# Local attention on one core: both band copies on VectorE, both probability scalings on GpSimd, the logarithm and exponential of the lengths moved behind the next tile's squares

## What is computed

```python
h = shift_token(x)
q, k, v = split(h @ wqkv)                    # 8 heads of 64
q, k = l2norm(q) * qs, l2norm(k) * ksc       # t / |t|
q, k = rotary_xpos(q, k)
sim = einsum(8 * q, look_around(k))          # windows of 64, this one and the one before
sim = where(i < j or i > j + 64 or j == -1, -big, sim)
attn = softmax(sim)
x = x + (attn @ look_around(v)) @ wo
# then a gated feed-forward layer with a layer norm ahead of it
```

## Time and profile before

| | us |
|---|---|
| median of three runs | 2175.28 |
| the profiled execution | 2175.47 |
| its span, first to last instruction | 2173.7 |
| PE busy | 2061.9 (95%) |
| DVE busy | 1712.6 (79%) |
| ACT busy | 1567.4 (72%) |
| POOL busy | 1514.7 (70%) |

### The profile page before, as it was taken

How to read it: one execution, slowest core, us unless ns; L and a number is a source line. 1 busy time by engine, 2 the same in 40 slices (tenths; PEclk the granted TensorE clock), 3 DMA queues, 4 the chain that set the end, 5 groups by cost and what they waited for, 6 DMA issues and landing times.

```text
span 2173.7 us, 53335 instructions
## 1 busy us (share of the span) xinstructions
PE 2061.9 (95%) x18830; PEld 1419.0 (65%) x18846; DVE 1712.6 (79%) x4035; ACT 1567.4 (72%) x4511; POOL 1514.7 (70%) x1837
## 2 busy tenths in 40 slices
PE   6999889999999999899999999999999989999988
PEld 4777657776567776565666666665777756677755
DVE  6787679998579999667766777677999956999965
ACT  3665569999459999436566556656999954999962
POOL 6788878887157777358787787876887833777742
PEclk9999999999999999999999999999999999999999
DMA  4000012112211121121121121210112121111211
GB/s 122 1 1 1 7 22 45 39 31 50 52 28 42 39 49 43 49 71 55 42 59 32 50 60 40 57 28 21 33 39 46 43 51 26 39 40 41 46 36 51
DMA packets 121369, 88.35 MB, mean 41 GB/s; under 512 B 85561, under 2 KB 102161, under 8 KB 118801
## 3 DMA queue, kind: packets, MB, share of 16 engines
q1 hardware_dynamic: 118544, 82.69, 15.8%
q10 hardware_dynamic: 2560, 2.24, 0.4%
HBM read 30.38 MB, written 8.39 MB: 18 GB/s over the span
## 4 chain that ended last, share of the span: by engine, by line
PE 60%; POOL 11%; DVE 11%; issue 7%; ACT 5%; SPq 4%; DMA 2%; POOLq 0%; ACTq 0%; DVEq 0%
PE bank L1379 11%; PE bank L620 7%; PE bank L1390 5%; PE bank L1370 5%; PE bank L687 5%; PE bank L662 4%; PE bank L633 4%; PE bank L675 4%; PE bank L695 3%; PE bank L750 3%; PE bank L627 3%; SPq L475 3%; POOL store L1178 2%; ACT store L874 2%; PE bank L758 2%
## 5 line engine op out<-in xcount | busy, mean ns | idle before, releaser
L1486 ACT ACTIVATE store<-bank 128x512 f32<-128x512 f32 x512 | 286.9, 600 | 201.6 <-PE bank L1379 198.4
L1533 DVE CUSTOM_DVE_ANT_0 store<-bank,store 128x512 f32<-128x512 f32 x512 | 335.7, 688 | 119.7 <-PE bank L1370 66.7
L1606 POOL TENSOR_SCALAR store<-store 128x512 f32<-128x512 f32 x512 | 349.6, 697 | 108.2 <-DVE store L1533 106.6
L874 ACT ACTIVATE store<-bank,store 128x128 f32<-128x128 f32 x1024 | 365.5, 385 | 16.7 <-DVE store L1030 16.3
L1178 POOL TENSOR_TENSOR store<-store 128x512 f32<-128x512 f32 x254 | 318.1, 1273 | 31.8 <-DVE store L1019 27.4
L1191 POOL TENSOR_TENSOR store<-store 128x512 f32<-128x512 f32 x256 | 261.8, 1044 | 111.5 <-ACT store L513 111.5
L1379 PEld LDWEIGHTS bank<-store 128*128 128x128 f32 x2048 | 239.8, 141 | 133.6 <-ACT store L1486 75.7
L1379 PE MATMUL bank<-store 128*128 128x128 f32 x2048 | 298.5, 277 | 0.0
L620 PE MATMUL bank<-store 128*128 128x512 f32 x496 | 234.8, 594 | 3.2 <-DVE store L1019 3.0
L874 ACT ACTIVATION_READ_ACCUMULATOR store<-bank,store 128x1 f32 x1024 | 228.9, 224 | 0.0
L1182 POOL TENSOR_TENSOR store<-store 128x512 f32<-128x512 f32 x128 | 133.3, 1041 | 126.4 <-DVE store L1035 126.4
(11 more groups left out here) (229 smaller groups left out, 4577.3 us busy)
## 6 DMA issues: line engine op xcount, KB each, us to landing
store<-store SPq DMA_DIRECT2D x256, 128.0 KB, 2.4
store<-parts SPq DMA_DIRECT2D x96, 192.0 KB
parts<-store SPq DMA_DIRECT2D x16, 384.0 KB, 3.6
store<-store SPq DMA_DIRECT2D x128, 32.0 KB
store<-store SPq DMA_DIRECT2D x128, 31.8 KB
store<-store SPq DMA_DIRECT2D x32, 127.0 KB
store<-in_L_ffn_wqkv_dram SPq DMA_DIRECT2D x4, 768.0 KB, 4.2
out_dram<-store SPq DMA_DIRECT2D x8, 256.0 KB, 2.4
```

The source lines that it names most:

```text
L874: last = nc.scalar.activation(prob[:, e, b, :], bank[3 + e][:, b * P:(b + 1) * P], ACT.Exp, bias=nmax[:, e, b:b + 1], accum_out=psums[:, e ...
L1486: nc.scalar.activation(AT[:, h % 4, c, :], bank[SCORE_BANKS + (64 * q + 4 * h + c) % TURN_BANKS][:, :], ACT.Exp, scale=-1.0).then_inc(aexp ...
L1533: nc.vector.tensor_tensor_reduce(out=S[:, h % 4, t, :], in0=bank[(64 * q + 4 * h + t) % SCORE_BANKS][:, :], in1=decay[:, off:off + L], sca ...
L1606: nc.gpsimd.tensor_scalar(s_, s_, -1.0, amax[:, h % 4, t:t + 1], ALU.mult, ALU.add).then_inc(shifted_done, 1)
```

## The change

Three steps. ScalarE no longer writes the band of bank 3; VectorE writes both bands, one after the other, behind `inverse_sums(j, 1)`. VectorE no longer scales the odd heads' probabilities; GpSimd scales both halves, the second one between `add_turned` and `clip_lengths` of `finish_qk`. And `inverse_lengths(j+2)`, which stood at the end of tile j, now stands in tile j+1 between `squares(j+3)` and `exps(j+1, 0)`.

```diff
@@ ScalarE
-            def write_band(q, j):
-                act.wait_ge(exp_done, 8 * q + 2 * j + 1)
-                nc.scalar.activation(bank[3][:, :], band_b[...], ACT.Copy).then_inc(band_at[0], 1)
...
+                    lengths = (q, j + 1) if j < 3 else (q + 1, 0)
+                    if (j == 0 and not before) or (j == 3 and not more):
+                        lengths = None
                     if more or j < 2:
                         ahead = (q, j + 2) if j < 2 else (q + 1, j - 2)
                         squares(*ahead)
+                    if lengths:
+                        inverse_lengths(act, *lengths)
                     exps(q, j, 0)
...
                         copy_v(*ahead)
-                    if more or j < 3:
-                        write_band(*((q, j + 1) if j < 3 else (q + 1, 0)))
                     copy_pT(q, j, 0)
-                    if more or j < 2:
-                        inverse_lengths(act, *ahead)
@@ VectorE
-            def scale_probs(q, j, e):
-                dve.wait_ge(pinv_done[e], 4 * q + j + 1)
-                nc.vector.tensor_tensor(prob[:, e, :, :], ...).then_inc(scaled_p[e], 1)
-            def write_band(q, j):
-                dve.wait_ge(exp_done, 8 * q + 2 * j + 2)
-                nc.vector.tensor_copy(bank[4][:, :], band_b[...]).then_inc(band_at[1], 1)
+            def write_band(q, j, e):
+                dve.wait_ge(exp_done, 8 * q + 2 * j + e + 1)
+                nc.vector.tensor_copy(bank[3 + e][:, :], band_b[...]).then_inc(band_at[e], 1)
...
                     inverse_sums(q, j, 1)
                     if more or j < 3:
-                        write_band(*((q, j + 1) if j < 3 else (q + 1, 0)))
-                    scale_probs(q, j, 1)
+                        write_band(*((q, j + 1) if j < 3 else (q + 1, 0)), 0)
+                        write_band(*((q, j + 1) if j < 3 else (q + 1, 0)), 1)
@@ GpSimd
-            def scale_probs(q, j):
+            def scale_probs(q, j, e):
...
             def finish_qk(q, j, first=False, added=False, between=None):
                 if not added:
                     add_turned(q, j, 0)
                     add_turned(q, j, 1)
+                if between:
+                    scale_probs(*between, 1)
                 if not first:
                     clip_lengths(q, j)
...
-                    scale_probs(q, j)
+                    scale_probs(q, j, 0)
                     if more or j < 2:
-                        finish_qk(*((q, j + 2) if j < 2 else (q + 1, j - 2)))
+                        finish_qk(*((q, j + 2) if j < 2 else (q + 1, j - 2)), between=(q, j))
+                    else:
+                        scale_probs(q, j, 1)
```

More of the change, by code:

```diff
@@ L876, in exps @@
                 last.then_inc(exp_done, 1)
-            def write_band(q, j):
-                act.wait_ge(exp_done, 8 * q + 2 * j + 1)
-                nc.scalar.activation(bank[3][:, :], band_b[:, 0 if j else 2, :, :].rearrange("p b w -> p (b w)"),
-                                     ACT.Copy).then_inc(band_at[0], 1)
             def copy_pT(q, j, e):
@@ L1035, in inverse_sums @@
                 nc.vector.reciprocal(pinv[:, e, :], psums[:, e, :]).then_inc(pinv_done[e], 1)
-            def scale_probs(q, j, e):
-                dve.wait_ge(pinv_done[e], 4 * q + j + 1)
-                nc.vector.tensor_tensor(prob[:, e, :, :], prob[:, e, :, :], bc(pinv[:, e, :], 2, P), ALU.mult).then_inc(scaled_p[e], 1)
-            def write_band(q, j):
-                dve.wait_ge(exp_done, 8 * q + 2 * j + 2)
-                nc.vector.tensor_copy(bank[4][:, :], band_b[:, 0 if j else 2, :, :].rearrange("p b w -> p (b w)")).then_inc(band_at[1], 1)
+            def write_band(q, j, e):
+                dve.wait_ge(exp_done, 8 * q + 2 * j + e + 1)
+                nc.vector.tensor_copy(bank[3 + e][:, :], band_b[:, 0 if j else 2, :, :].rearrange("p b w -> p (b w)")).then_inc(band_at[e], 1)
             def add_out(s, q, j):
@@ L1178, in add_turned @@
                 nc.gpsimd.tensor_tensor(straight[:, at, :], straight[:, at, :], turned[:, at, :], ALU.add).then_inc(add_done, 1)
-            def scale_probs(q, j):
-                pool.wait_ge(pinv_done[0], 4 * q + j + 1)
-                nc.gpsimd.tensor_tensor(prob[:, 0, :, :], prob[:, 0, :, :], bc(pinv[:, 0, :], 2, P), ALU.mult).then_inc(scaled_p[0], 1)
+            def scale_probs(q, j, e):
+                pool.wait_ge(pinv_done[e], 4 * q + j + 1)
+                nc.gpsimd.tensor_tensor(prob[:, e, :, :], prob[:, e, :, :], bc(pinv[:, e, :], 2, P), ALU.mult).then_inc(scaled_p[e], 1)
             def normalize(q, j, i):
@@ L1198, in clip_lengths, with finish_qk @@
                 nc.gpsimd.tensor_scalar(flat, flat, 1e-24, None, ALU.max).then_inc(clip_done, 1)
-            def finish_qk(q, j, first=False, added=False):
+            def finish_qk(q, j, first=False, added=False, between=None):
                 if not added:
```

## The result

| | before | after |
|---|---|---|
| median of four runs each, side by side | 2175.61 | 2188.89 |
| lowest and highest | 2174.26, 2177.27 | 2188.59, 2189.79 |
| the profiled execution | 2175.47 | 2189.15 |
| its span | 2173.7 | 2187.0 |
| mean granted clock of TensorE | 0.996 | 0.992 |

A forecast was written before the change was run, and what follows sets the result against it. The prediction took a ring of waits through ScalarE and TensorE, 7.94 us per tile, to bound the kernel. Its terms, -4.6 + 8.4 + 2.2 - 0.8 = +5.2 us, gave 2180.5, range 2169 to 2190.

The forecast's parts named there:

- What bounds the tile: Ordinary tile: a ring of waits sets its 7.94 us, and TensorE's 0.17 idle ahead of the scores awaits ScalarE's band copy.
- both rings: Two loops of waits, each 7.94 us: one through ScalarE's copy_pT and first exponential, one through its band copy and the scores.
- Ordinary tiles, -4.6: 92 tiles away from layers' starts, ends and the power: each gains 0.05 us, 4.6 us in all.
- ScalarE's ring: Loop from copy_pT through the first exponential, weigh_values and prob_transpose: shrinks from 7.94 to 7.89 us.
- Rival 2: Ordinary tiles: the scores' ring rules and weigh_values waits for VectorE; tile 7.77 us, total 2169.5; chance 0.08.
- rival 3: GpSimd becomes the pacemaker: second scaling 1.25 us, clip still 0.68; total 2188, or 2197 without slack; chance 0.12.
- The band copies hidden: VectorE's second band copy ends at 709.21, wanted at 709.33: 0.1 us of slack, so no cost.
- Logarithm at 1.45, clip at 0.25, scaling at 1.04: Ordinary tile: logarithm starts 1.45 us after copy_pT; on GpSimd the clip takes 0.25 and the second scaling 1.04.
- The 12 tiles, 8.82 and +8.4: Tiles with the layer norm's power: late clip delays the logarithm; 8.82 us against 8.15, 8.4 us lost in all.
- Rival 1: Tiles with the layer norm's power: the late clip costs no more than before; total 2170 to 2172; chance 0.17.
- Layers' ends, +2.2: Last tile's odd scaling and the power for ff_normalize come later on GpSimd: +0.55 us each, 2.2 in all.
- Layers' starts, -0.8: VectorE, 0.6 us lighter, gives back an estimated 0.2 us at each layer's start, 0.8 in all.

The follow-up runs named there:

- p1_bands: Kernel before the change, with only the band copies changed: VectorE writes both bands, ScalarE none; 2175.69 us, ratio 1.0003.
- x5_twice: Changed kernel with TensorE's transposition for the next sequence, just ahead of the score products, done twice; 2196.95 us in a single run.
- x1_power: Changed kernel with the layer norm's addition and power on GpSimd moved between the clip and the two normalize of tile 1; 2175.8 us, ratio 0.9992.
- p3_scale: Kernel before the change, with only the odd heads' scaling moved from VectorE to GpSimd; 2202.55 us in a single run.
- x6_fill: Changed kernel with 16 additional, unread transpositions on TensorE ahead of the last tile's weigh_values of each layer; 2185.51 us, ratio 1.0035.
- x2_ends: Changed kernel, but VectorE scales the odd heads' probabilities again in the last two tiles of each layer; 2181.47 us, ratio 1.0015.
- x4_nolog: Changed kernel without the logarithm and exponential of the lengths, ScalarE only passing the signal on; 2177.18 us in a single run.

## Why the prediction was right or wrong

- **What bounds the tile: wrong.** The step that failed is the reading of the 0.17 us ahead of the scores as a wait for ScalarE's band copy. It is a fixed distance between TensorE's last transposition and the scores: with the band 0.47 early it stayed (p1_bands), and one more load ahead of it came on top (x5_twice). The ring that sets the pace is the scores' own: scores, maxima, exponential (1.86 from the scores' loads), 1.39, 0.72, 2.90, then 0.76 to the last transposition's load and 0.31 to the next scores: 7.94. Its waits were in the earlier trace rows. I had both rings at 7.94, and let the second shrink by an idle time that can't shrink. TensorE's own order is not the pace either: in the tile of x1_power that starts at 440.39 its transpositions ahead of `weigh_values` (L633) start 0.17 later than a tile before, and the loads of `weigh_values` stay at 3.97. In p3_scale's tile from 711.92 they come at 4.21, with `copy_pT` later by as much (3.48 instead of 3.25) and `add_out` done at 3.82 as ever: they wait for ScalarE, as I had taken it.
- **Ordinary tiles, -4.6: mis-sized.** ScalarE's ring did become shorter: where the maxima are early, in a tile with the power, the first exponential follows L511 by 422.04 - 421.68 = 0.36, so that the stretch is the predicted 1.45 + 0.36 = 1.81. But the ring was not alone. In an ordinary tile the exponential still starts at 1.87 (709.89 - 708.02), with the maxima, so 92 x 0.05 was not gained. The tiles gave 0.4 us in all. Rival 2 named the right ring with the wrong consequence, 7.77: its 0.17 was the same fixed distance, and its condition, `weigh_values` waiting for VectorE, doesn't hold. My list gave 7.94 to rival 3, which the clip's 0.25 excludes.
- **The band copies hidden: right**, with 0.47 us between their end and the scores' loads. My 0.1 was the same distance less 0.17, by which the scores were never going to start earlier, and less 0.19 for the way to TensorE.
- **Logarithm at 1.45, clip at 0.25, scaling at 1.04: right.** The trace has 1.45, 0.25 and 1.05. The clip comes 0.54 into the tile (708.56 - 708.02; predicted start 0.62). Here the Trainium skill (SBUF — State Buffer, "SBUF: two separate sides") is borne out once more: the clip took 0.68 beside VectorE's scaling and takes 0.25 where that is gone. Rival 3 fell with it, since the band copies don't hold GpSimd's additions up.
- **The 12 tiles, 8.82 and +8.4: right.** They take 8.79 to 8.82, +8.0 in all, with L511 at 2.40 behind `copy_pT` and waiting for the clip. x1_power shows it by taking the power away from that place. That the length agrees to 0.01 is in part luck, as the ordinary 7.89 that it was built on was not met. Rival 1, the absorbed power, fell.
- **Layers' ends, +2.2: right in sign, too small, by another path.** They cost 3.6 up to the last down projection. I had the late power of the earlier `ff_normalize` as an upper bound only, and followed the last one. The earlier one has the maxima of the last tile behind it, hence exponentials, transposition and TensorE. And I had nothing for the clock, which x6_fill puts at some 1.5 us. Without it 2.1 is left, but that this is near 2.2 is luck: rid of the waits (x2_ends) the ends are 2.5 us shorter than before the change, a gain that I had nowhere, and the waits cost 4.6.
- **Layers' starts, -0.8:** -0.4 measured.
- **Not in the sum: 1.7 us at the start and 0.6 behind the second layer**, both in code that is unchanged. Ahead of the first scores the clock was at its lower level for 17.0 us in this execution (from 40.8, 238.8 and 272.9) and for 10.2 in the one before the change. The same code reached the first scores anywhere from 295.6 to 299.4 in the runs above, so a profiled pair can differ by this alone. All four runs of the changed kernel had a mean clock of 0.991 or 0.992, the twenty of x2_ends and x6_fill 0.994 to 0.996, so much of the difference comes with the layers' ends. Whether the rest is chance is left open.

The terms against the measured ones: -4.6 came out as -0.4, +8.4 as +8.0, +2.2 as +3.6, -0.8 as -0.4. That is +5.2 against +10.8, and 0.2, 1.7 and 0.6 on top. Half of the miss is the ring, a sixth the ends, and more than a quarter unchanged code. The time came out 1.1 us below the top of the range, in the part that rival 3 had put there (2188) by a mechanism that didn't occur. That it lies inside the range is therefore in part luck.

## What to carry to other kernels

Before an idle gap is counted as a gain, look whether it has the same length in every tile and whether its releaser ended well ahead. Such a gap may be the engine's own, and a ring that runs through it can't get shorter by it. An engine's idle time is a buffer for the work that comes only now and then: whoever fills it must find that work another place, here ahead of a wait that exists anyway. At the ends of loops follow each engine's order from the late instruction on, since there the next thing in the queue decides.

## What was not expected of the hardware

- The 0.17 us between the last 128-row load and the first 64-row load: 0.17 ahead of L662 in the ordinary tiles of every kernel here, whatever was ready. The change back, ahead of L675, shows the same 0.17 where nothing else is waited for, in the loads of the changed kernel. That the change of rows is what takes the time was not tested by itself. The row:

```profile
709.06 0.42 PEld L675 LDWEIGHTS bank<-store 128*128 128x128 f32 x4 [0.17 <-issue]
```

- An idle stretch of 2.2 us of TensorE was followed by 3.4 us at the clock's lower level at three of four layer ends, and at 10 of 16 in the four kernels that have it; with the idle time filled it stayed at the higher one. The changed kernel's fourth end had no fall and cost 0.3.
- A signal that ScalarE only passes on (x4_nolog) isn't held up by activations that stand ahead of it and still run: `normalize` started at 743.03, while they ran from 742.64 to 743.72, about 1.1 us earlier in the tile than behind the logarithm.
- GpSimd takes 1.04 us for the power of 128x4 numbers, as long as for a product of 128x512.
